# A graph-attention layer on one core: b1 and b2 spread by TensorE, the second table built before the third tile's masks, half of its scaled x on GpSimd

## The chip, the cores and the metric

The kernel runs on one core of a Trainium2 chip. The time is the device time of one execution in microseconds (us). Below, PE is TensorE, DVE is VectorE, ACT is ScalarE, POOL is GpSimd and SP is SyncE, whose queue only starts transfers here.

## The reference, cut to what matters

```python
in_fts = W @ x.T                                  # x: (4096, 128) f32, W: (128, 128)
f1 = (w1 @ in_fts).T + b1                         # (4096, 1)
f2 = (w2 @ in_fts).T + b2                         # (4096, 1)
logits = f1 + f2.T                                # (4096, 4096)
bias = where(adj > 0, 0.0, -1e9)                  # adj: (4096, 4096) int32
coefs = softmax(leaky_relu(logits) + bias, axis=-1)
out = layernorm(x + coefs @ x)                    # (4096, 128) f32, eps 1e-5
```

The adjacency matrix is 64 MiB of int32 and is read once; it is by far the largest operand.

## The kernel before, in words

**The algebra.** The exponential of the leaky ReLU of f1+f2 is exp(f1)exp(f2) where f1+f2 is positive, and exp(0.01 f1)exp(0.01 f2) where it is not. So no 4096 x 4096 matrix of exponentials is made. Two tables are: table 1 holds x scaled by exp(0.01 f2), table 0 holds x scaled by exp(f2), each with the scale itself as one more column, and each as a high f16 half and a low f16 half (258 columns for one block of 128 columns of adj). The coefficients are two masks: mask 1 for the edges of negative sum, mask 0 for those of positive sum. PE multiplies masks by tables.

**A tile** is 128 rows of adj (4096 columns), 32 tiles in all, in slots 0 to 3 (`QT` = 4); four tiles are a quad. For each tile:
- SP and ACT load it (`load_near`, `load_far`: two transfers of 512 KB each). A slot's next load waits for the cast of the tile that is in it (`cast_done`).
- DVE `cast` (L683) makes int8 of the int32 adjacency. ACT `signs` (L445, four activations) writes the signs of f1+f2. DVE `combine` (L688) joins both, DVE `turn` (L696) transposes the mask in blocks of 32 and so gives mask 1, DVE `plus` (L701) makes mask 0.
- PE `edge_sums` (L1002): 32 matmuls of mask 1 with table 1 and 32 of mask 0 with table 0. `turn` of tile t waits for the sums of tile t-4.
- ACT `evacuate` brings the sums out of PSUM. For each quad DVE `moments`, POOL `rows` and ACT `normalise` finish the softmax, the residual and the layer norm, and POOL stores the rows.

**The set-up** ahead of this loop is written out by hand: each engine's list of instructions in the order in which it runs them. x comes in four chunks (`load_x`, `xl_in[h]`). POOL loads w1 and w2 (L340, L341), which PE turns into columns (L969) and multiplies with W (L972, L973). b1 and b2 are loaded by POOL to all 128 partitions (L346, L347). PE transposes x (`turn_x`) and makes f1 (`f1_columns`). DVE makes f2 (`xv_product`, `f2_sum`, one chunk of it on ACT in `f2_sums`), adds b2 (L726), and spreads it as rows (`f2_rows`, L637). `stat_max` and `stat_out`, with PE's `turn_stats` and `widen_stats`, find maxima over all rows.
For each table and each of the four chunks of x: `scale_x` (DVE L667) multiplies the chunk by the scale; `split_x` (ACT L503) writes the high half; `low_x` (DVE L673) the low half. The scaled chunk lies in one buffer, `ybuf`, for both tables: table 0's chunk can be scaled when `low_x` of table 1's has run. Table 0's chunks 0 and 1 are scaled by DVE, 2 and 3 by ACT (`scale_act`, L483: 16 activations).
DVE's order from the first mask on is: mask of tile 0 between the chunks of table 1; `cast`, `combine`, `turn` of tile 1; `cast` and `combine` of tile 2; `scale_x(0, 0)`, `scale_x(0, 1)`, `turn(2, 2)`; `plus` of tiles 0, 1 and 2 between `low_x` of table 0's chunks 0, 1 and 2; tile 3's `cast`, `combine`, `turn`; `low_x(0, 3)`; `plus(3, 3)`.

**The flag.** POOL computes the row factors and then a flag that says whether the fast path may be used (L368 to L392), once the second maxima are there (`gst_ready`). Every engine waits for the flag (`fast`) before it starts with tile 4, so tile 4's `signs` and `cast` come after it. The fast path is the one that runs.

Of the kernel before, what the change touches and what calls it, by code (L numbers as in the profile page):

```python
# [42 lines left out]
def gat_kernel(nc, x, adj, W, w1, b1, w2, b2, out):  # L43
# [24 lines left out]
    with ExitStack() as ctx:  # L68
# [83 lines left out]
        FIRST = 3  # L152
# [124 lines left out]
        def _(sp):  # L277
# [9 lines left out]
            sp.dma_start(wsb[0:P // 2, :], W[0:P // 2, :]).then_inc(w_in, 16)  # L287
            for a in range(A // 2):
                load_x(sp, a, 0)
            for h in range(1, BCH):  # L290
# [47 lines left out]
        def _(pool):  # L338
            pool.memset(ident[:, :], 0.0).then_inc(ident_zero, 1)
            pool.dma_start(wrow[0:1, :], w1).then_inc(w12_in, 16)  # L340
            pool.dma_start(wrow[1:2, :], w2).then_inc(w12_in, 16)  # L341
# [4 lines left out]
            pool.dma_start(b12[:, 0:1], b1.partition_broadcast(P)).then_inc(b12_in, 16)  # L346
            pool.dma_start(b12[:, 1:2], b2.partition_broadcast(P)).then_inc(b12_in, 16)  # L347
# [84 lines left out]
        def _(act):  # L432
            act.dma_start(wsb[P // 2:P, :], W[P // 2:P, :]).then_inc(w_in, 16)
            for h in range(BCH):
                for a in range(A // 2, A):
# [20 lines left out]
            def f2_sums(n0, n1):  # L456
                act.wait_ge(xv_ready, 1)
                for n in range(n0, n1):
                    ins = act.activation(junk[:, n * D:(n + 1) * D], xv[:, n * D:(n + 1) * D], ACT.Copy, accum_out=f2raw[:, n:n + 1])
                ins.then_inc(f2raw_act, 1)  # L460
# [69 lines left out]
            load_far(3, 3)  # L530
            xT_out(6)
            split_x(1, 0)
            xT_out(7)
# [92 lines left out]
        def _(dve):  # L626
# [97 lines left out]
            dve.wait_ge(f2raw_act, 2)
            dve.wait_ge(b12_in, 32)
            dve.tensor_scalar(f2l[:, :], f2raw[:, :], b12[:, 1:2], None, ALU.add).then_inc(f2l_ready, 1)  # L726
            dve.wait_ge(f2l_ready, 1)
# [3 lines left out]
            stat_max(0, 0, 2)  # L731
            dve.wait_ge(consts_ready, 2)
            spread_f1(0, 0, FIRST * KB, 6, 256)
            stat_out(0, 0, 2)
            dve.tensor_scalar(nF2[:, :], gst[:, 0:1], -1.0, None, ALU.mult).then_inc(nF2_ready, 1)
# [382 lines left out]
```

## Time and profile before

| | us |
|---|---|
| median of 3 runs | 285.12 (284.54 to 285.3) |
| profiled execution, its own time | 286.38 |
| its span, first to last instruction | 284.7 |

| engine | busy us | share | instructions |
|---|---|---|---|
| PE matmul | 260.4 | 91% | 2161 |
| DVE | 247.1 | 87% | 320 |
| ACT | 198.3 | 70% | 300 |
| POOL | 70.6 | 25% | 93 |

The mean granted TensorE clock is 0.974 of full. A row of the timeline has start, duration, engine, line, operation, output<-input, shape and count; instructions of one kind that follow each other are merged in one row, and in brackets stand the idle time ahead of it and what ended that.

### The profile page before, as it was taken

What the parts mean: (1) busy time and instruction counts of PE and PEld (TensorE: products, weight loads), DVE (VectorE), ACT (ScalarE), POOL (GpSimd) and SP (SyncE); (2) the same over time, 40 slices, a digit from 0 to 9 for tenths busy, and PEclk for the clock granted to TensorE, in tenths of its full rate; (3) what the DMA queues carried; (4) which work ended last, traced back from release to release, by engine and by line L of the source; (5) the groups of instructions that cost most, each with busy time, mean ns of one, the idle gap of its engine ahead of it and who ended that gap; (6) DMA issues with size and microseconds to landing.
All of it is one profiled execution on the core that took longest, in us unless ns stands there. A gap on an engine that the chain in (4) does not pass through costs nothing.

```text
span 284.7 us, 5940 instructions
## 1 busy us (share of the span) xinstructions
PE 260.4 (91%) x2161; PEld 225.9 (79%) x2161; DVE 247.1 (87%) x320; ACT 198.3 (70%) x300; POOL 70.6 (25%) x93
## 2 busy tenths in 40 slices
PE   0969959799999999999999999999999999999970
PEld 0959846588888888888888888888888888888850
DVE  1878997993997799999999999999999999999862
ACT  2679799936999999699389928991999196113210
POOL 5000004491000003300460056006500650065340
PEclk9999996799999999999999999999999999999996
DMA  5899999999999999999999999999999999501031
GB/s 169 232 287 315 326 316 268 289 281 235 210 268 328 324 326 322 242 314 334 329 294 345 322 322 249 330 340 342 226 327 323 323 249 342 149 0 37 1 90 23
DMA packets 22702, 73.64 MB, mean 259 GB/s; under 512 B 3232, under 2 KB 4384, under 8 KB 22688
## 3 DMA queue, kind: packets, MB, share of 16 engines
q1 hardware_dynamic: 11280, 35.17, 42.5%
q10 hardware_dynamic: 9936, 34.64, 41.3%
q0 software_dynamic: 1472, 3.67, 4.9%
q8 instruction: 6, 0.10, 0.2%
q14 instruction: 8, 0.07, 0.1%
HBM read 71.37 MB, written 2.10 MB: 258 GB/s over the span
## 4 chain that ended last, share of the span: by engine, by line
DVE 59%; DMA 10%; issue 10%; ACT 8%; POOL 5%; PE 3%; ACTq 2%; DVEq 1%; POOLq 0%
DVE mn L683 19%; DVE msk L696 11%; DVE mn L688 10%; DMA nat<-in_adj 7%; ACT sgn L445 6%; DMA msk<-in_x 3%; DVE post L802 3%; DVE ybt L817 2%; PE ps L1002 2%; DVE bns L822 2%; DVE post L804 2%; DVE ntot L807 2%; DVE bt L673 1%; ACTq L268 1%; POOL mrow L371 1%
## 5 line engine op out<-in xcount | busy, mean ns | idle before, releaser
L1002 PE MATMUL ps<-bt,msk 128*128 128x258 f16 x2048 | 236.0, 277 | 5.2 <-DVE msk L696 5.2
L1002 PEld LDWEIGHTS ps<-bt,msk 128*128 128x128 fp8e5 x2048 | 203.2, 99 | 37.5 <-issue 5.5
L445 ACT ACTIVATE sgn<-f2b,nf1l 128x1024 int8<-128x1024 f32 x128 | 136.6, 1144 | 5.7 <-POOL flag L392 4.4
L683 DVE TENSOR_SCALAR mn<-nat 128x4096 int8<-128x4096 int32 x32 | 73.0, 2282 | 7.0 <-DMA nat<-in_adj 4.3
L399 POOL TENSOR_SCALAR nmr<-mv 128x4 f32<-128x4 f32 x7 | 12.6, 1801 | 150.6 <-DVE mv L826 150.6
L688 DVE SCALAR_TENSOR_TENSOR mn<-sgn,mn 128x1024 uint32<-128x1024 uint32 x32 | 39.2, 1225 | 3.4 <-ACT sgn L445 2.4
L696 DVE STREAM_TRANSPOSE msk<-mn 128x1024 uint32<-128x1024 uint32 x32 | 39.8, 1245 | 2.6
L576 ACT ACTIVATE post<-ps,ac 128x258 f32<-128x258 f32 x64 | 26.5, 467 | 22.1 <-PE ps L1002 22.1
L583 ACT ACTIVATE ybt<-ybt,nmr,rstd 128x128 f32<-128x128 f32 x28 | 11.5, 483 | 34.1 <-POOL nmr L404 34.1
L701 DVE TENSOR_SCALAR msk<-msk 128x1024 uint32<-128x1024 uint32 x32 | 22.2, 695 | 1.0
L410 POOL DMA_DIRECT2D out<-ybt x24 | 21.7, 911 | 4.0 <-issue 3.8
L962 PEld LDWEIGHTS ps<-vsb,xn 128*128 128x128 f32 x64 | 14.4, 332 | 0.5 <-issue 0.4
L962 PE MATMUL ps<-vsb,xn 128*128 128x1 f32 x64 | 14.0, 342 | 0.0
L363 POOL DMA_DIRECT2D xn<-in_x x4 | 3.2, 797 | 39.8 <-DVE mn L683 39.8
L673 DVE SCALAR_TENSOR_TENSOR bt<-bt,post 128x1024 f16<-128x1024 f16 x8 | 9.8, 1219 | 0.7 <-ACT bt L503 0.7
L503 ACT ACTIVATE bt<-post 128x1024 f16<-128x1024 f32 x8 | 8.4, 1053 | 2.2 <-DVE post L667 2.1
L817 DVE SCALAR_TENSOR_TENSOR ybt<-ntot,rec,xn 128x128 f32<-128x128 f32 x28 | 8.0, 346 | 1.8 <-DVE rec L811 1.7
L802 DVE TENSOR_TENSOR post<-post 128x1032 f32<-128x1032 f32 x7 | 8.6, 1226 | 0.0
L953 PE MATMUL ps<-ident,msk 128*128 128x128 f32 x32 | 8.5, 427 | 0.0
L400 POOL TENSOR_SCALAR vpe<-mv 128x4 f32<-128x4 f32 x7 | 7.4, 1055 | 0.4
L402 POOL TENSOR_TENSOR rstd<-vpe,mhalf 128x4 f32<-128x4 f32 x7 | 7.3, 1046 | 0.6
L667 DVE TENSOR_TENSOR post<-msk,cs 128x1024 f32<-128x1024 f32 x6 | 7.3, 1213 | 0.0
(106 smaller groups left out, 107.3 us busy)
## 6 DMA issues: line engine op xcount, KB each, us to landing
nat<-in_adj SPq DMA_DIRECT2D x64, 512.0 KB, 13.2
nat<-in_adj ACTq DMA_DIRECT2D x64, 512.0 KB, 16.1
xn<-in_x POOLq DMA_DIRECT2D x4, 512.0 KB, 19.5
out<-ybt POOLq DMA_DIRECT2D x24, 64.0 KB, 7.7
msk<-in_x ACTq DMA_DIRECT2D x8, 128.0 KB, 5.9
msk<-in_x SPq DMA_DIRECT2D x8, 128.0 KB, 4.3
out<-ybt SPq DMA_DIRECT2D x4, 64.0 KB, 2.2
out<-post SPq DMA_DIRECT2D x16, 16.0 KB, 1.5
```

Of the source, the lines that this page charges most:

```text
L410: pool.dma_start(out_g[q, g], ybt[g * SQ:(g + 1) * SQ, s]).then_inc(out_stored[s], 16)
L445: ins = act.activation(sgn[:, c, g * JA:(g + 1) * JA], f2b[:, :], ACT.Sign, bias=nf1l[:, bass.ds(G * t + g, 1)], scale=-1.0)
L576: ins = act.activation(post[:, s, m, c, :], ps[:, 2 * c + m, 0:2 * DV], ACT.Copy, scale=ac[:, m, bass.ds(QT * q + c, 1)])
L673: dve.scalar_tensor_tensor(out=btv[m][:, part, DV:DV + D], in0=btv[m][:, part, 0:D], scalar=-LOW, in1=ybuf[:, h], op0=ALU.mult, op1=ALU.ad ...
L683: dve.tensor_scalar(mn[:, c % 2], nat[:, c], 0, EDGE, ALU.is_gt, ALU.mult).then_inc(cast_done, 1)
L688: dve.scalar_tensor_tensor(out=mn_w[c % 2], in0=sgn_w[c], scalar=MINUS, in1=mn_w[c % 2], op0=ALU.bitwise_xor, op1=ALU.bitwise_and).then_in ...
L696: dve.transpose(turned[c].rearrange("p (b g s) -> p g b s", b=NB, g=G), mn_w[c % 2].rearrange("p (g b r) -> p g b r", g=G, b=NB)).then_inc ...
L701: dve.tensor_scalar(plus_w[c], turned[c], PLUS, 1, ALU.bitwise_and, ALU.logical_shift_right).then_inc(plus_ready, 1)
L802: dve.tensor_tensor(post[:, s, 0], post[:, s, 0], post[:, s, 1], ALU.add).then_inc(sums_added, 1)
L817: dve.scalar_tensor_tensor(out=ybt[:, s, c, :], in0=ntot[:, c, 0:D], scalar=rec[:, c:c + 1], in1=xn[:, bass.ds(QT * q + c, 1), :].rearrang ...
L962: ins = pe.matmul(ps[:, bank, at:at + 1], xT[:, n * P:(n + 1) * P], vsb[:, D:D + 1], start=True, stop=True)
L1002: ins = pe.matmul(ps[:, 2 * c + m, 0:2 * DV], mask_f[c][m][:, n // KB, n % KB, :], btv[m][:, n, :], start=(n == 0), stop=(n == NK - 1))
```

## The change

- w1 and w2 are loaded on ACT's queue ahead of its x chunks; W is one transfer on SP's queue. b1 and b2 are loaded by POOL to one partition (`brow`), and PE spreads them with a matmul by a row of ones; DVE copies the result (`b12`).
- `f1_columns` of the first two blocks (`FIRST` = 2, was 3) multiplies with both vectors, so f2 of chunk 0 comes from PE too; DVE's product and ACT's eight sums for that chunk (`f2_sums`) are gone.
- In the set-up, the first exponential on ACT comes ahead of `square(2)`, the second one behind `signs` of tile 0; DVE runs `spread_f1` of the first rows ahead of `f2_rows`, and `scale_x(1, 1)` ahead of tile 0's cast.
- Table 0's chunks 0 and 1 are scaled by POOL (one 128x1024 multiplication each, signal `y_act`), 2 and 3 by DVE; `scale_act` is gone.
- Table 0 is finished (DVE and ACT) before `cast`, `combine` and `turn` of tile 2 and `signs` of tile 2 begin. PE runs mask 0 of tiles 0 and 1 with all of table 0, and then mask 1 and mask 0 of tile 2.
- POOL's load of x by rows (`xn`) waits for the cast of tile 1, was that of tile 2.

```diff
-        FIRST = 3
+        FIRST = 2
+        F2_AT = FIRST * KB
...
-            pool.dma_start(wrow[0:1, :], w1).then_inc(w12_in, 16)
-            pool.dma_start(wrow[1:2, :], w2).then_inc(w12_in, 16)
+            pool.dma_start(brow[:, 0:1], b1.partition_broadcast(1)).then_inc(brow_in, 16)
+            pool.dma_start(brow[:, 1:2], b2.partition_broadcast(1)).then_inc(brow_in, 16)
...
-            pool.dma_start(b12[:, 0:1], b1.partition_broadcast(P)).then_inc(b12_in, 16)
-            pool.dma_start(b12[:, 1:2], b2.partition_broadcast(P)).then_inc(b12_in, 16)
...
+            pool.wait_ge(cs_ready[0], 1)
+            for h in range(2):
+                pool.wait_ge(table_ready[1], h + 1)
+                part = slice(h * CN, (h + 1) * CN)
+                pool.tensor_tensor(ybuf[:, h], xl_chunk(h), cs[:, 0, part, None].to_broadcast([P, CN, D]),
+                                   ALU.mult).then_inc(y_act, 1)
...
-            pool.wait_ge(cast_done, 3)
+            pool.wait_ge(cast_done, 2)
...
@@ ACT, after signs of tile 1 @@
-            rows_out()
-            signs(2, 2, between=next_tile)
-            square(3)
-            act.wait_ge(nf1l_ready, 2)
-            signs(3, 3, between=lambda: split_x(0, 0))
-            act.wait_ge(cast_done, 3)
-            load_far(QT + 2, 2)
-            split_x(0, 1)
-            scale_act(2)
-            split_x(0, 2)
-            scale_act(3)
-            split_x(0, 3)
+            square(3)
+            rows_out()
+            split_x(0, 0)
+            act.wait_ge(cast_done, 2)
+            load_far(QT + 1, 1)
+            split_x(0, 1)
+            split_x(0, 2)
+            split_x(0, 3)
+            act.wait_ge(nf1l_ready, 2)
+            signs(2, 2)
+            signs(3, 3, between=next_tile)
...
@@ DVE, after combine of tile 1 @@
-            turn(1, 1)
-            cast(2, 2, 0)
             dve.wait_ge(f1n_ready, G)
             dve.tensor_reduce(stat[:, 2:3], f1n[:, :], AX_X, ALU.max, apply_absolute_value=True)
-            combine(2, 2)
             dve.wait_ge(squares_ready, BCH)
             dve.tensor_reduce(stat[:, 3:4], squares[:, :], AX_X, ALU.add).then_inc(stat_ready, 1)
+            turn(1, 1)
             dve.wait_ge(cs_ready[0], 1)
             low_den(0)
-            scale_x(0, 0)
+            scale_x(0, 2)
             stat_max(1, 2, 4)
-            scale_x(0, 1)
-            dve.wait_ge(y_ready[0], 2)
-            turn(2, 2)
+            scale_x(0, 3)
             plus(0, 0)
             low_x(0, 0)
+            plus(1, 1)
             stat_out(1, 2, 4)
-            plus(1, 1)
             low_x(0, 1)
-            plus(2, 2)
             low_x(0, 2)
+            low_x(0, 3)
+            cast(2, 2, 0)
+            combine(2, 2)
+            dve.wait_ge(y_act, 2)
+            turn(2, 2)
+            plus(2, 2)
             cast(3, 3, 0)
             combine(3, 3)
-            dve.wait_ge(y_act, 2)
+            dve.wait_ge(y_ready[0], 2)
             turn(3, 3)
-            low_x(0, 3)
             plus(3, 3)
...
@@ PE, after the first table-1 sums @@
-            edge_sums(1, 1)
-            turn_stats(1, 2, 4)
+            edge_sums(1, 1, 0, NK // 2)
             widen_stats(1, 2, 4)
-            pe.wait_ge(turn_done, 3)
-            edge_sums(2, 1)
+            edge_sums(1, 1, NK // 2, NK)
             pe.wait_ge(den_ready[0], 1)
             pe.wait_ge(xeps_ready, 1)
-            plus_sums(0, range(2))
-            plus_sums(1, range(2))
-            plus_sums(0, [2])
-            plus_sums(1, [2])
-            plus_sums(2, range(3))
+            for h in range(BCH):
+                plus_sums(h, range(2))
+            pe.wait_ge(turn_done, 3)
+            edge_sums(2, 1)
+            for h in range(BCH):
+                plus_sums(h, [2])
```

## Rows read from the trace of the kernel before

**Rows 1.** Windows: from:to, length, busy us (count) by engine, clock, DMA share, GB/s.
```profile
60.00:80.00 20.00, 20.00 (x181) 17.46 (x180) 15.07 (x13) 14.01 (x18) 4.76 (x13) 1.00 1.03 238
```
**Rows 2.** Timeline of the last 35 us: PE's last row, DVE's last `plus`.
```profile
249.79 25.78 PE L1002 MATMUL ps<-bt,msk 128*128 128x258 f16 x229
...
260.72 0.69 DVE L701 TENSOR_SCALAR msk<-msk 128x1024 uint32<-128x1024 uint32 x1
```
**Rows 3.** Timeline of PE alone, 36 to 60 us.
```profile
36.83 2.46 PE L1002 MATMUL ps<-bt,msk 128*128 128x258 f16 x16
42.41 6.46 PE L1002 MATMUL ps<-bt,msk 128*128 128x258 f16 x32 [3.12 <-DVE msk L696]
...
52.09 8.11 PE L1002 MATMUL ps<-bt,msk 128*128 128x258 f16 x59 [2.12 <-DVE msk L696]
```
**Rows 4.** Windows of PE alone: busy us (count), clock, DMA share, GB/s.
```profile
52.00:54.00 2.00, 1.91 (x10) 0.50 1.04 295
```
**Rows 5.** Costliest groups: line, operation, count | busy us, mean ns | idle before.
```profile
L683 DVE TENSOR_SCALAR mn<-nat 128x4096 int8<-128x4096 int32 x32 | 73.0, 2282 | 7.0 <-DMA nat<-in_adj 4.3
...
L688 DVE SCALAR_TENSOR_TENSOR mn<-sgn,mn 128x1024 uint32<-128x1024 uint32 x32 | 39.2, 1225 | 3.4 <-ACT sgn L445 2.4
L696 DVE STREAM_TRANSPOSE msk<-mn 128x1024 uint32<-128x1024 uint32 x32 | 39.8, 1245 | 2.6
...
L701 DVE TENSOR_SCALAR msk<-msk 128x1024 uint32<-128x1024 uint32 x32 | 22.2, 695 | 1.0
...
L673 DVE SCALAR_TENSOR_TENSOR bt<-bt,post 128x1024 f16<-128x1024 f16 x8 | 9.8, 1219 | 0.7 <-ACT bt L503 0.7
L503 ACT ACTIVATE bt<-post 128x1024 f16<-128x1024 f32 x8 | 8.4, 1053 | 2.2 <-DVE post L667 2.1
...
L667 DVE TENSOR_TENSOR post<-msk,cs 128x1024 f32<-128x1024 f32 x6 | 7.3, 1213 | 0.0
```
**Rows 6.** Timeline of DVE's set-up, 15 to 70 us.
```profile
15.13 1.23 DVE L629 TENSOR_TENSOR sgn<-msk,vsb 128x1024 f32<-128x1024 f32 x1 [0.83 <-DMA msk<-in_x]
...
18.11 2.00 DVE L637 STREAM_TRANSPOSE f2b<-f2l 128x1024 f32<-128x1024 f32 x1
...
21.73 1.22 DVE L667 TENSOR_TENSOR post<-msk,cs 128x1024 f32<-128x1024 f32 x1
...
23.27 2.29 DVE L683 TENSOR_SCALAR mn<-nat 128x4096 int8<-128x4096 int32 x1 [0.34 <-DMA nat<-in_adj]
...
29.80 1.24 DVE L696 STREAM_TRANSPOSE msk<-mn 128x1024 uint32<-128x1024 uint32 x1
...
37.44 2.29 DVE L683 TENSOR_SCALAR mn<-nat 128x4096 int8<-128x4096 int32 x1
...
66.57 2.29 DVE L683 TENSOR_SCALAR mn<-nat 128x4096 int8<-128x4096 int32 x1 [2.66 <-issue]
```
**Rows 7.** Timeline of ACT at 18.8 us.
```profile
18.77 0.21 ACT L521 ACTIVATE de<-f2l 128x32 f32<-128x32 f32 x1
```
**Rows 8.** Timeline of the first 7 us, PE.
```profile
6.43 0.23 PE L969 MATMUL ps<-ident,wrow 2*128 2x2 f32 x1 [6.43 <-DMA wrow<-in_L_gnn_w]
```
**Rows 9.** Timeline of POOL alone, 0 to 66 us.
```profile
2.95 0.31 POOL L344 TENSOR_SCALAR_AFFINE_SELECT ident<-ident 128x128 f32<-128x128 f32 x1
...
53.92 2.35 POOL L368 TENSOR_SCALAR gsum<-f1n,gst 128x32 f32<-128x32 f32 x1 [5.67 <-DVE gst L662]
...
56.45 3.18 POOL L371 TENSOR_SCALAR mrow<-gsum 128x32 f32<-128x32 f32 x1
...
61.23 0.25 POOL L377 TENSOR_TENSOR ea<-ea,mrow 128x32 f32<-128x32 f32 x1
61.44 0.19 POOL L379 TENSOR_TENSOR rng<-gst 128x1 f32<-128x1 f32 x1
...
65.21 0.30 POOL L392 TENSOR_SCALAR flag<-rng 128x1 int32<-128x1 f32 x1
```
**Rows 10.** Loads of adj issued from 45 to 60 us.
```profile
DMA to landing us min/median/max: 16.6/20.5/24.5
```

More of the change, by code:

```diff
@@ L285, in load_tile @@
                 load_near(QT * q + c, c)
[L287 to L290, printed above, removed]
+            sp.dma_start(wsb[:, :], W).then_inc(w_in, 16)
+            for h in range(BCH):
                 for a in range(A // 2):
@@ L436, in _ @@
                     load_x(act, a, h)
+                if h == 1:
+                    act.wait_ge(consts_ready, 1)
+                    act.activation(ac[:, 0, 0:1], ones[:, 0:1], ACT.Copy)
             def load_far(t, c):
@@ L454, in xT_out @@
                                accum_out=xt8[:, b:b + 1]).then_inc(xT_ready, 1)
[L456 to L460, printed above, removed]
             def square(h):
                 act.wait_ge(xl_in[h], 16 * A)
-                if h == 0:
-                    act.wait_ge(f2raw_act, 2)
-                else:
+                if h:
                     act.wait_ge(squares_ready, h)
@@ L530, in _ @@
             load_far(3, 3)
+            split_x(1, 0)
             xT_out(6)
-            split_x(1, 0)
-            xT_out(7)
+            act.wait_ge(nF2_ready, 1)
+            act.activation(be[:, :], f2l[:, :], ACT.Exp, bias=nF2[:, 0:1]).then_inc(exp_ready, 1)
+            scales(0, be)
             split_x(1, 1)
@@ L715, in _ @@
             dve.wait_ge(vsb_ready, 1)
-            xv_product(0)
             xv_product(1)
             f2_sum(1)
+            dve.wait_ge(b12_made, 1)
+            dve.tensor_copy(b12[:, :], ps[:, 6, D + 2:D + 4]).then_inc(b12_ready, 1)
             xv_product(2)
             f2_sum(2)
+            dve.wait_ge(b12_ready, 1)
+            dve.wait_ge(f1_made, 1)
+            dve.tensor_scalar(f2l[:, 0:F2_AT], ps[:, 0, F2_AT:2 * F2_AT], b12[:, 1:2], None,
+                              ALU.add).then_inc(f2l_ready, 1)
+            dve.wait_ge(consts_ready, 2)
+            spread_f1(0, 0, FIRST * KB, 0, 0)
             xv_product(3)
@@ L723, in _ @@
             dve.wait_ge(f2raw_ready, BCH - 1)
[L724 to L727, printed above, removed]
+            dve.tensor_scalar(f2l[:, F2_AT:], f2raw[:, F2_AT:], b12[:, 1:2], None, ALU.add).then_inc(f2l_ready, 1)
+            dve.wait_ge(f2l_ready, 2)
             dve.tensor_reduce(stat[:, 0:1], f2l[:, :], AX_X, ALU.max)
@@ L730, in _ @@
             f2_rows()
[L731 to L735, printed above, removed]
             dve.wait_ge(nf1_made, 1)
@@ L740, in _ @@
             scale_x(1, 0)
+            stat_max(0, 0, 2)
+            scale_x(1, 1)
+            stat_out(0, 0, 2)
+            dve.tensor_scalar(nF2[:, :], gst[:, 0:1], -1.0, None, ALU.mult).then_inc(nF2_ready, 1)
             cast(0, 0, 0)
             low_den(1)
-            scale_x(1, 1)
             combine(0, 0)
@@ L977, in _ @@
             f1_columns(0)
+            pe.wait_ge(brow_in, 32)
+            pe.matmul(ps[:, 6, D + 2:D + 4], ones[0:1, :], brow[:, :], start=True, stop=True).then_inc(b12_made, 1)
             turn_x(2)
@@ L981, in _ @@
             f1_columns(2)
-            turn_stats(0, 0, 2)
-            turn_x(4)
-            widen_stats(0, 0, 2)
             pe.wait_ge(alike_ready, 1)
@@ L989, in _ @@
                       stop=True).then_inc(nf1_made, 1)
+            turn_x(4)
+            turn_stats(0, 0, 2)
             f1_columns(3)
+            widen_stats(0, 0, 2)
             turn_x(5)
@@ L1040, in _ @@
             edge_sums(2, 1)
-            pe.wait_ge(den_ready[0], 1)
-            pe.wait_ge(xeps_ready, 1)
-            plus_sums(0, range(2))
-            plus_sums(1, range(2))
-            plus_sums(0, [2])
-            plus_sums(1, [2])
-            plus_sums(2, range(3))
+            for h in range(BCH):
+                plus_sums(h, [2])
             pe.wait_ge(gst_ready, 2)
@@ L1053, in _ @@
             edge_sums(3, 1)
-            plus_sums(3, range(3))
             for h in range(BCH):
```

64 lines of the change are left out of this document (31 added, 33 removed).

## The prediction

> **What bounds the kernel now.** I read the windows first, then the end of the timeline, then PE's restart, then the set-up's order. In a window of the main loop PE is busy all of its 20 us at full clock, and the DMA engines are full too [rows 1]. At the end DVE has made its last mask at 260.72 + 0.69 = 261.4, while PE works until 249.79 + 25.78 = 275.57 [rows 2]: a backlog of 14 us. The chain of waits names DVE most, because `turn` waits for sums of four tiles before, but what sets the end is PE. PE's last idle time of its own ends at 52.09 [rows 3]; from there it never stops. By the program 64 matmuls of L1002 lie before 52.09 (mask 1 of tiles 0 and 1; 16 + 32 of them are in the first two of [rows 3]), so 1984 of 2048 lie behind it. The clock was 0.50 until about 54 [rows 4], which costs half of 2 us. So one matmul takes (275.57 - 52.09 - 1.0)/1984 = 0.1121 us, a tile of 64 takes 7.17.
>
> So the question is when PE's unbroken stretch starts and how much is left then. I count from the start of tile 2's mask-1 sums in the new order, where 2048 - 128 = 1920 matmuls are left: 1920 x 0.1121 = 215.2 us. Before, that much was left at 275.57 - 215.2 = **60.35**. Call the same point after S. The time changes by S - 60.35, if nothing starves PE later. The tail behind 275.57 is untouched. The profiled execution took 286.38 us with a span of 284.7; the median of the runs is 285.12, and I apply the difference to the median.
>
> **The front, to tile 1's cast.** PE's first instruction waited until 6.43 for w1 and w2 [rows 8]. On ACT's queue they come earlier, by some 2 us, and the spread of b1 and b2 is one matmul and one copy. I cost all this at nothing: DVE's f2 of the last chunk starts at 15.13 when x lands [rows 6], and that covers it. If the cover were gone it would be worth 2 us at most. ACT's x loads are issued one descriptor list later (some 0.5 us); if x lands later by that, it is a loss of 0 to 0.5, taken as 0. W as one transfer changes nothing that is waited for.
>
> From 15.13 the sums and maxima are as before, so `f2_rows` ends at 18.11 + 2.00 = 20.1 [rows 6]. The first exponential started at 18.77 behind `square(2)` [rows 7]; it now runs at 18.0, so `scale_x(1, 0)` starts at 20.35 and not at 21.73 [rows 6]. Two `scale_x` (1.21 each) and the maxima (about 0.9) then bring DVE to 23.65 for tile 0's cast, which could not start before 23.27, when its load landed [rows 6]. Most of the gain is then given back: `combine(0)` waits for `signs` of tile 0, which starts 1.4 us earlier but now has PE's `turn_x(5)` behind `widen_stats` in its middle; I get 26.5 for its end, and 26.5 to 27.55 for `split_x(1, 0)` (1.05, [rows 5]). `low_x(1, 0)` follows (1.22), and `turn(0)` starts at 28.9, before at 29.80 [rows 6]. Then the same list as before, with ACT's second exponential (0.8) now in the way of `split_x(1, 3)`: tile 1's cast would start at **37.0**, before at 37.44 [rows 6].
>
> **POOL's two multiplications.** No POOL instruction of this size is in the trace. From `affine_select`, 0.31 for 128 elements [rows 9], 1024 elements would take 2.5; from 0.25 for 32 elements against 0.19 for one [rows 9], 0.19 + 1024 x 0.0019 = 2.1. I take 2.2 each. The first can start when the second exponential and `low_x(1, 0)` are done, at 29.0; the second after `low_x(1, 1)`. What they do to DVE the trace shows from one side only: L368 (32 elements) took 2.35 and L371 3.18 where the neighbour of the same size, L377, took 0.25 [rows 9], and in their time DVE ran `low_x`, `plus` and `cast` at their usual durations. So POOL waits for DVE whole instructions long. Whether DVE waits for POOL no row shows; the bounds are 0 and all of the 2 x 2.2 us. I take the same whole-instruction wait, since it is the only kind of conflict the rows have. During `turn` and the reductions POOL went on (L377 at 61.23 lies in tile 3's `turn` and took its 0.25, [rows 9]), so those cover it. The first runs 29.0 to 31.2, covered by `turn(0)` to 30.15: `scale_x(1, 2)` starts 1.0 late. The second gets in at 36.0, between `low_x(1, 2)` and `spread_f1`, is covered for 0.45 and delays `low_x(1, 3)` to 38.2. Tile 1's cast then starts at **39.4**: 2.4 behind 37.0 and 2.0 behind today's.
>
> The Trainium skill ("SBUF — State Buffer", section "SBUF: two separate sides") has the shared port pair as an exclusive lock held for a whole instruction by whichever of the two started first. By that rule the sum is the one just made; by bandwidth sharing it would lie between this and rival A. The rows agree for POOL's half of it. The skill's "GPSIMD Engine Reference", section 3, gives 4497 ns for a two-input add of 2048 elements; an estimate from it is 2.2 us for 1024.
>
> **From tile 1's cast to S.** DVE in order: cast 2.28, combine 1.23, two small reductions 0.3, turn 1.25, `low_den` 0.3, `scale_x` 1.21, `stat_max` 0.5, `scale_x` 1.21, plus 0.69, `low_x` 1.22, plus 0.69, `stat_out` 0.15, three `low_x` 3.66, then tile 2's cast 2.28, combine 1.23, turn 1.25 [rows 5]. Sum 19.5. The small reductions wait for ACT's rows, behind `signs(1)` and `square(3)`; ACT has them out by 41.5, in time. ScalarE loses its 16 scaling activations, which were off the path. S = 39.4 + 19.5 = **58.9**. PE must have done mask 0 of tiles 0 and 1 by then: table 0's first chunk is ready at 49.6 and the last at 54.1, and 64 matmuls at 0.112 take 7.2, so PE is through by 58. It works at half clock from turn(1) on for about 6 us, as in the row of 42.41 (6.46 us for 32) [rows 3], and that is covered, as it was before. `turn(3)` ends 5.5 after S, PE needs it at S + 7.17.
>
> **Behind S.** PE needs tile 4's `turn` at S + 14.34 = 73.2 (before: 74.7). Tile 4 hangs on the flag: flag at 65.51 [rows 9], four `signs`, `combine`, `turn` gave 73.36, that is flag + 7.86. POOL's chain now starts at S - 8.5 = 50.4 and meets three `low_x` and a cast, 5.9 us in which it stands still; then `turn(2)` and `turn(3)` let it through. I get the flag at S + 6.4 = 65.3, `turn(4)` at 73.2: just in time, 0.0 to 0.3 late. Tile 4's cast waited for the flag too, at 66.57 [rows 6]. Tile 2's cast moves from 42.2 to some 54.2, so tile 6's loads are issued 12 us later on SP's and ACT's queues, at 56.5. PE needs that mask at S + 28.7, DVE must begin it by 82.8: 26 us, against 24.5 for the slowest load of that stretch [rows 10]. Just covered. The load `xn` is issued a few us earlier, nobody waits for it before 100.
>
> **The sum:** S 58.9 against 60.35 is -1.45, the flag +0.15: **-1.3 us, 283.8 us**. This case's own range is 282.7 to 284.9.
>
> **Rivals.**
> A. DVE does not wait for POOL. Then cast(1) starts at 37.0, S = 56.5, -3.8 us: 281.3. For it: POOL's instructions never lengthened a DVE instruction in the trace. Against: none of them was longer than 0.3 us of own work. Chance 0.20.
> B. The other side: the flag becomes the bound. Its chain of 18 small POOL instructions took from 53.92 to 65.51 [rows 9], with DVE idle or in port-free work for much of the last 4 us. It now sits between the back-to-back `low_x`, casts and combines. If one more cast (2.3 us) gets ahead of it, the flag comes at 68, `turn(4)` ends at 75.9, and PE starts tile 4 1.2 us later than before: 286.3. It decides from a flag at 66.8 on (no gain), and from 67.7 on the kernel is slower by 0.3%. Tile 6's load coming 2 us late would look alike in time but not in place. Chance 0.18.
> C. The change does not do what it says: x lands 0.5 late and POOL's multiplications take 3 us, so each stall grows by 0.8; S is 61, flat: 284.4 to 285.9, centre 285.4. Chance 0.17.
>
> **How the numbers follow.** Forecast 0.45, A 0.20, B 0.18, C 0.17. A measurement here tells about 0.3%, 0.86 us, from no change. The forecast lies beyond that with seven eighths of its chance; with A that is 0.59 faster. Same: the rest of the forecast, most of C, some of B: 0.23. Slower: B's larger part: 0.18. The range takes in A and B: 281.2 to 286.5.
>
> **What would show it.** `scale_x(1, 2)` (the third L667 of the set-up) starting over 1 us behind `turn(0)`, while a POOL multiplication ends at its start, shows the stall; back to back shows A. The start of tile 1's cast near 39.4, `turn(2)` ending near 58.9 with PE idle 1 us or less before it, and PE without idle from there on, show the sum. A gap in PE at tile 4 (near 73) with ACT's `signs` behind L392 shows B; a gap at tile 6 shows the load. It is wrong if PE's mask-0 sums of tiles 0 and 1, at half clock, end behind `turn(2)`.

## The result, and the profile after

The changed kernel takes **280.75 us** (median; 280.48 to 282.38), beside 285.21 (284.54 to 287.0) for the kernel before on the same chip: a ratio of 0.985, interval 0.981 to 0.990. A second measurement on another chip gave 0.981 (0.977 to 0.985). The forecast of 283.8 had the right sign and was too small by 3 us, and 280.75 lies below its range.

The profiled execution has a span of 278.8 us and 280.48 us as its own time, 5.9 less than that of before. The medians differ by 4.5, because before's profiled execution was 1.2 above its median. So single times of the traces explain the gain up to about 1.4 us, not better.

First, three groups of the changed kernel's page, as in [rows 5].

```profile
L363 POOL TENSOR_TENSOR post<-msk,cs 128x1024 f32<-128x1024 f32 x2 | 4.7, 2352 | 24.5 <-DVE bt L664 24.5
...
L664 DVE SCALAR_TENSOR_TENSOR bt<-bt,post 128x1024 f16<-128x1024 f16 x8 | 11.3, 1433 | 0.0
...
L658 DVE TENSOR_TENSOR post<-msk,cs 128x1024 f32<-128x1024 f32 x6 | 8.1, 1351 | 0.0
```

The mean of `low_x` rose from 1219 ns to 1433 and that of `scale_x` from 1213 to 1351 [rows 5]: 8 x 0.214 + 6 x 0.138 = 2.5 us.

Next, PE alone in the changed kernel, which answers to [rows 2, 3], and its windows (columns as in [rows 4]).

```profile
35.41 3.09 PE L1003 MATMUL ps<-bt,msk 128*128 128x258 f16 x16
...
40.92 3.60 PE L1003 MATMUL ps<-bt,msk 128*128 128x258 f16 x16 [0.87 <-DVE msk L687]
...
44.96 224.73 PE L1003 MATMUL ps<-bt,msk 128*128 128x258 f16 x2000
```

```profile
44.00:46.00 2.00, 2.00 (x10) 0.50 1.03 270
46.00:48.00 2.00, 2.00 (x19) 0.94 1.01 274
```

PE's unbroken stretch starts at 44.96, before at 52.09. Of its 2000 matmuls 80 lie ahead of tile 2's. Counted back from 44.96 + 224.73 = 269.69, the other 1920 begin at 269.69 - 215.2 = **54.5** = S. It was 60.35 before and was forecast at 58.9. The 215.2 us for 1920 matmuls can be checked in e6 below, where PE waits right ahead of tile 2's sums and so shows them as one row (in brackets the wait for `turn(2)`):

```profile
53.20 214.96 PE L1008 MATMUL ps<-bt,msk 128*128 128x258 f16 x1920 [1.28 <-DVE msk L692]
```

The clock column has PE at the lower level (0.50) until about 46.

DVE's set-up in the changed kernel, in start times, answers to [rows 6]:

```profile
12.88 1.22 DVE L620 TENSOR_TENSOR sgn<-msk,vsb 128x1024 f32<-128x1024 f32 x1
...
17.73 1.21 DVE L658 TENSOR_TENSOR post<-msk,cs 128x1024 f32<-128x1024 f32 x1
...
20.83 2.29 DVE L674 TENSOR_SCALAR mn<-nat 128x4096 int8<-128x4096 int32 x1
...
26.25 1.24 DVE L687 STREAM_TRANSPOSE msk<-mn 128x1024 uint32<-128x1024 uint32 x1
27.41 2.05 DVE L658 TENSOR_TENSOR post<-msk,cs 128x1024 f32<-128x1024 f32 x1
29.39 1.22 DVE L664 SCALAR_TENSOR_TENSOR bt<-bt,post 128x1024 f16<-128x1024 f16 x1
30.52 1.21 DVE L658 TENSOR_TENSOR post<-msk,cs 128x1024 f32<-128x1024 f32 x1
31.66 2.92 DVE L664 SCALAR_TENSOR_TENSOR bt<-bt,post 128x1024 f16<-128x1024 f16 x1
...
35.92 2.28 DVE L674 TENSOR_SCALAR mn<-nat 128x4096 int8<-128x4096 int32 x1
...
53.10 1.25 DVE L687 STREAM_TRANSPOSE msk<-mn 128x1024 uint32<-128x1024 uint32 x1
...
67.66 1.25 DVE L687 STREAM_TRANSPOSE msk<-mn 128x1024 uint32<-128x1024 uint32 x1
```

And POOL alone in the changed kernel: its two multiplications and the flag.

```profile
26.49 1.90 POOL L363 TENSOR_TENSOR post<-msk,cs 128x1024 f32<-128x1024 f32 x1 [22.24 <-DVE bt L664]
30.68 2.81 POOL L363 TENSOR_TENSOR post<-msk,cs 128x1024 f32<-128x1024 f32 x1 [2.30 <-DVE bt L664]
...
60.77 0.30 POOL L399 TENSOR_SCALAR flag<-rng 128x1 int32<-128x1 f32 x1
```

Step by step, with start times:

| step | before | forecast | measured |
|---|---|---|---|
| last f2 product | 15.13 | 15.13 | 12.88 |
| `scale_x(1, 0)` | 21.73 | 20.35 | 17.73 |
| tile 0's cast | 23.27 | 23.65 | 20.83 |
| `turn(0)` | 29.80 | 28.9 | 26.25 |
| tile 1's cast | 37.44 | 39.4 | 35.92 |
| S | 60.35 | 58.9 | 54.5 |
| flag done | 65.51 | S + 6.4 | S + 6.6 |

The first rows are 2.3 to 2.8 us ahead of the forecast. Behind `turn(0)` some 0.8 us more comes in up to tile 1's cast, and 0.9 from there to S, so that S is 4.4 ahead. The larger part is there before `turn(0)`. So the first question for the experiments was: what moved the front?

The row to look at is the share of time in which the DMA engines were busy, while x lands. The kernel before, DMA view of the first 12 us in 40 slices of 0.3 us (each digit tenths), then the changed kernel:

```profile
DMA  0000000056957999999998943122557999999999
...
msk<-in_x ACTq DMA_DIRECT2D x8, 128.0 KB, 5.9
...
b<-in_L_gnn_b POOLq DMA_DIRECT2D x2, 0.5 KB, 6.1
```

```profile
DMA  0000000659878989999999999999999999999999
...
msk<-in_x ACTq DMA_DIRECT2D x8, 128.0 KB, 4.3
...
brow<-in_L_gnn_b POOLq DMA_DIRECT2D x2, 0.0 KB, 3.4
```

Before, from 6.9 to 9.0 us the engines fell to 1 to 5 tenths with all of x and the first masks still to come. In the changed kernel there is no dip. The last number of the load rows is us from issue to landing.

### The profile page after: what moved, and what is told of

It reads as the page before. It is cut to its first block, busy times and chain, and to the rows that moved or that the text cites. A ratio compares the mean times of both kernels' runs of the same rounds, so it can differ in the third digit from the quotient of the medians.

```text
span 278.8 us, 5912 instructions
## 1 busy us (share of the span) xinstructions
PE 259.6 (93%) x2163; PEld 225.5 (81%) x2163; DVE 248.3 (89%) x321; ACT 191.0 (69%) x268; POOL 78.3 (28%) x93
## 4 chain that ended last, share of the span: by engine, by line
DVE 66%; issue 9%; DMA 8%; POOL 6%; ACT 5%; ACTq 2%; DVEq 1%; PE 1%; POOLq 0%
DVE mn L674 20%; DVE msk L687 11%; DVE mn L679 11%; DMA nat<-in_adj 7%; ACT sgn L456 5%; DVE post L797 3%; DVE bt L664 2%; DVE ybt L812 2%; DVE post L658 2%; DVE bns L817 2%; DVE post L799 2%; DVE ntot L802 2%; DMA msk<-in_x 2%; DVE f2raw L624 1%; DVE sgn L620 1%
## 5 line engine op out<-in xcount | busy, mean ns | idle before, releaser
L456 ACT ACTIVATE sgn<-f2b,nf1l 128x1024 int8<-128x1024 f32 x128 | 136.6, 1147 | 10.3 <-POOL flag L399 6.4
L567 ACT ACTIVATE post<-ps,ac 128x258 f32<-128x258 f32 x64 | 26.6, 469 | 19.3 <-PE ps L1003 19.2
L417 POOL DMA_DIRECT2D out<-ybt x24 | 22.3, 935 | 3.4 <-issue 3.3
L363 POOL TENSOR_TENSOR post<-msk,cs 128x1024 f32<-128x1024 f32 x2 | 4.7, 2352 | 24.5 <-DVE bt L664 24.5
L664 DVE SCALAR_TENSOR_TENSOR bt<-bt,post 128x1024 f16<-128x1024 f16 x8 | 11.3, 1433 | 0.0
L960 PEld LDWEIGHTS ps<-vsb,xn 128*128 128x128 f32 x48 | 10.9, 332 | 0.3 <-ACT xn L464 0.3
L960 PE MATMUL ps<-vsb,xn 128*128 128x1 f32 x48 | 10.4, 338 | 0.2 <-ACT xn L464 0.2
L464 ACT ACTIVATE xn<-ps 128x512 f32<-128x512 f32 x8 | 4.7, 592 | 5.1 <-PE ps L948 5.1
L658 DVE TENSOR_TENSOR post<-msk,cs 128x1024 f32<-128x1024 f32 x6 | 8.1, 1351 | 0.0
```

What stands on the lines that cost most here:

```text
L417: pool.dma_start(out_g[q, g], ybt[g * SQ:(g + 1) * SQ, s]).then_inc(out_stored[s], 16)
L456: ins = act.activation(sgn[:, c, g * JA:(g + 1) * JA], f2b[:, :], ACT.Sign, bias=nf1l[:, bass.ds(G * t + g, 1)], scale=-1.0)
L567: ins = act.activation(post[:, s, m, c, :], ps[:, 2 * c + m, 0:2 * DV], ACT.Copy, scale=ac[:, m, bass.ds(QT * q + c, 1)])
L658: dve.tensor_tensor(ybuf[:, h], xl_chunk(h), cs[:, m, part, None].to_broadcast([P, CN, D]), ALU.mult).then_inc(y_ready[m], 1)
L664: dve.scalar_tensor_tensor(out=btv[m][:, part, DV:DV + D], in0=btv[m][:, part, 0:D], scalar=-LOW, in1=ybuf[:, h], op0=ALU.mult, op1=ALU.ad ...
L960: ins = pe.matmul(ps[:, 7, n - F2_AT:n - F2_AT + 1], xT[:, n * P:(n + 1) * P], vsb[:, D:D + 1], start=True, stop=True)
```

## The experiments

Two theories for the front (theory 1 and theory 2 in the expectations of e1 to e3). **Theory S**: the loads of b1 and b2 to 128 partitions, 256 elements of 4 bytes, hold the DMA engines up, and so hold x up. **Theory Q**: it is w1 and w2 on ACT's queue (PE's first matmul now at 3.38, before 6.43 [rows 8]). For the two multiplications of POOL, **theory L** (a lock for whole instructions, both ways) against **theory P** (DVE is not affected; the "rival P" in e6's expectation is another one, that PE sets the start of the unbroken stretch). Each chip of the experiments had its own runs of the kernel before, with medians from 285.88 to 286.28; numbers from different chips are compared by their ratio to it.

**e1: only b1 and b2 changed, in the kernel before.**

```diff
-pool.dma_start(b12[:, 0:1], b1.partition_broadcast(P))
-pool.dma_start(b12[:, 1:2], b2.partition_broadcast(P))
+pool.dma_start(brow[:, 0:1], b1.partition_broadcast(1))
+pool.dma_start(brow[:, 1:2], b2.partition_broadcast(1))
...
+pe.matmul(ps[:, 2, 0:2], ones[0:1, :], brow[:, :], start=True, stop=True)
+dve.tensor_copy(b12[:, :], ps[:, 2, 0:2])
```

> The kernel before, and only b1 and b2 changed: loaded to one partition instead of 128 and spread by a PE matmul and a DVE copy. x's last chunk lets DVE start its f2 product at 15.13 us in the trace before and at 12.88 in the changed kernel. Theory 1 (the two loads of b to 128 partitions, 4 bytes each, hold the DMA engines up at 6 to 10 us, where their share was 0.60 to 0.68): the product starts near 13, the DMA share at 6 to 10 us is over 1.0, and the time falls by 1.5 to 2.3 us, to some 283.3. Theory 2 (the earlier x comes from w1, w2 and W on other queues): the product stays at 15.1 and the time within 0.4 us of the kernel before.

**e2: the reverse, in the changed kernel** (POOL loads b1 and b2 to 128 partitions, PE's matmul and DVE's copy go).

> The changed kernel with b1 and b2 loaded to 128 partitions by GpSimd again, no spread by PE, all else as changed. Theory 1: the last f2 product goes back from 12.88 to about 15, the start of tile 1's cast from 35.9 to about 38, and 1.5 to 2.3 us of the gain of 4.4 are lost (282.3 to 283). Theory 2: nothing moves by more than 0.4 us.

e1 took 283.92 us, ratio 0.993 (0.989 to 0.996). e2 took 283.25, ratio 0.992 (0.989 to 0.994), where the changed kernel had 0.985 and 0.981. The windows (as in [rows 4], here with all engines) of e1, then of e2:

```profile
6.00:8.00 2.00, 1.44 (x7) 1.38 (x8) 0.31 (x2) 1.12 (x2) 0.00 (x0) 1.00 1.02 315
```

```profile
4.00:6.00 2.00, 0.30 (x3) 0.21 (x1) 0.29 (x1) 1.10 (x2) 0.20 (x1) 1.00 0.56 184
6.00:8.00 2.00, 1.75 (x8) 1.57 (x8) 0.00 (x0) 0.59 (x2) 0.00 (x0) 1.00 0.38 138
```

The dip is gone in e1 (share 1.02) and back in e2 (0.56 and 0.38), where POOL issues the loads. In e2 DVE's timeline has its first f2 product waiting 4.96 us for x; the second row is tile 1's cast, 1.8 us later than in the changed kernel:

```profile
9.59 1.23 DVE L617 TENSOR_TENSOR sgn<-msk,vsb 128x1024 f32<-128x1024 f32 x1 [4.96 <-DMA msk<-in_x]
...
37.71 2.28 DVE L671 TENSOR_SCALAR mn<-nat 128x4096 int8<-128x4096 int32 x1
```

So S holds in both directions. But in e1 the last f2 product moved only from 15.13 to 14.48, not to 12.88: something more is in the front.

**e3: w1 and w2 back on POOL's queue and W in halves, in the changed kernel.**

```diff
-act.dma_start(wrow[0:1, :], w1)
-act.dma_start(wrow[1:2, :], w2)
+act.dma_start(wsb[P // 2:P, :], W[P // 2:P, :])
...
+pool.dma_start(wrow[0:1, :], w1)
+pool.dma_start(wrow[1:2, :], w2)
```

> The changed kernel with w1 and w2 on GpSimd's queue ahead of b1 and b2, and W in two halves on SP's and ACT's queues, as in the kernel before. Theory 1: PE's first instruction goes from 3.4 back to about 6.4 us, hidden behind the x loads for most of it: DVE's last f2 product moves by 0 to 0.7 us, the time by 0 to 0.7. Theory 2: the product goes back to 15, the time rises by 2.

It took 282.45, ratio 0.989 (0.983 to 0.995): by the ratios 1.2 to 2.3 us more than the changed kernel, though the intervals overlap; S is at 55.87, 1.4 later. No dip in the DMA share (1.06 and over from 4 us on), yet the last f2 product came at 14.25, 1.4 later, and tile 0's cast at 23.02. Neither theory had this size: theory S expected 0 to 0.7 us, theory Q 2. What moved the cast stands in ACT's queue. The timeline of e3 has ACT's first transfer of tile 0's load and DVE's cast of that tile; then come the same issue in the kernel before, with the activation at its start, and both in the changed kernel:

```profile
8.12 0.65 ACTq L277 DMA_DIRECT2D nat<-in_adj  x1
...
23.02 2.30 DVE L675 TENSOR_SCALAR mn<-nat 128x4096 int8<-128x4096 int32 x1 [0.87 <-DMA nat<-in_adj]
```

```profile
8.93 0.60 ACT L453 ACTIVATE xn<-ps 128x512 f32<-128x512 f32 x1 [1.79 <-PE ps L953]
8.93 0.65 ACTq L274 DMA_DIRECT2D nat<-in_adj  x1
```

```profile
6.74 0.60 ACT L464 ACTIVATE xn<-ps 128x512 f32<-128x512 f32 x1 [1.63 <-PE ps L948]
6.75 0.70 ACTq L277 DMA_DIRECT2D nat<-in_adj  x1
```

ACT issues this load right at its first `xn` activation, which has waited for PE. With w1 and w2 late, PE is late, and so is the load. In e1 the issue was at 8.81 and the cast at 23.75, still waiting for the load. From this issue to the start of the cast it is 14.3 us before and 14.9 in e1 and e3; the whole front below has 14.1. So the landing of tile 0 follows PE's start. (No run moved this issue and nothing else; that it decides is read from these rows.)

**e5: the whole new front alone, in the kernel before** (b1 and b2 to one row, w1 and w2 on ACT's queue, W as one transfer, x chunks in order; nothing of the new order, no POOL multiplications).

> The kernel before, with all loads of the front as in the changed kernel (w1 and w2 on ACT's queue, W in one transfer, b1 and b2 to one partition and spread by PE), and its old order behind. Theory F (front and order each bring about half): against the kernel before it gains 2 to 2.8 us (283.3 or less where before is 285.9), since b alone gave 2.0; PE's unbroken stretch starts near 50.3. Rival (the order alone brings nearly all, and the front's gain is swallowed by the wait for tile 0's load, which b alone already met with 1.46 us of idle time): no more than 2.0, and DVE's wait for that load grows to 2 us.

It took 282.5, ratio 0.989 (0.985 to 0.993): 3.4 us, more than expected. PE's unbroken stretch starts at 48.38 (before 52.09), where 50.3 was expected. DVE's timeline, its last f2 product and tile 0's and tile 1's casts, 2.5, 2.3 and 2.6 us ahead of [rows 6]:

```profile
12.59 1.21 DVE L629 TENSOR_TENSOR sgn<-msk,vsb 128x1024 f32<-128x1024 f32 x1
...
20.96 2.29 DVE L683 TENSOR_SCALAR mn<-nat 128x4096 int8<-128x4096 int32 x1 [0.58 <-DMA nat<-in_adj]
...
34.82 2.29 DVE L683 TENSOR_SCALAR mn<-nat 128x4096 int8<-128x4096 int32 x1
```

**e9: the changed kernel with both front parts undone** (the edits of e2 and e3 together), which leaves the new order, the work moved off DVE for chunk 0, and POOL's multiplications.

> The changed kernel with both parts of its front undone (w1, w2 and the 128-row b1, b2 on GpSimd's queue, W in halves): what the new order, the shorter f2 and GpSimd's multiplications bring alone. The front alone brought 3.4 us of 285.9. Theory F (front and order add up): 1.0 to 2.2 us faster than the kernel before in the same job. Rival (they overlap, since both end at the wait for tile 0's load): over 3 us faster, or no faster at all.

It took 284.61, ratio 0.995 (0.991 to 0.998): 1.6 us. PE alone in e9 shows S at 58.10, and DVE's first f2 product waits for x:

```profile
58.10 4.08 PE L997 MATMUL ps<-bt,msk 128*128 128x258 f16 x35 [1.57 <-DVE msk L685]
```

```profile
11.43 1.23 DVE L618 TENSOR_TENSOR sgn<-msk,vsb 128x1024 f32<-128x1024 f32 x1 [3.88 <-DMA msk<-in_x]
```

e5's 1.1% and e9's 0.55% add up to 1.6%; the changed kernel gained 1.5% and 1.9%. But e9 is not quite "the order with the old front": its x landed later than before (DMA share 0.35 and 0.53 in 6:8 and 8:10 us, before 0.60 and 0.68), and its last f2 product came at 16.50, where it was 15.13. Against the changed kernel that is 3.6 us, and S differs by 3.6 us too.

**e10: b1 and b2 to 128 partitions again, but on ACT's queue ahead of its x chunks.** This asks whether GpSimd's queue has a part in the dip.

```diff
-pool.dma_start(b12[:, 0:1], b1.partition_broadcast(P))
-pool.dma_start(b12[:, 1:2], b2.partition_broadcast(P))
...
+act.dma_start(b12[:, 0:1], b1.partition_broadcast(P))
+act.dma_start(b12[:, 1:2], b2.partition_broadcast(P))
```

> The changed kernel with b1 and b2 loaded to all 128 partitions, but on ACT's queue behind w1 and w2 instead of GpSimd's. With them on GpSimd's queue the DMA share fell to 0.56 and 0.38 in 4:6 and 6:8 us. Theory K (GpSimd's queue, software-made packets, holds the DMA engines up): the share stays at 1.0 and the time is within 0.5 us of the changed kernel. Theory S (it is the 256 packets of 4 bytes, whichever queue they come from): the share falls below 0.8 in some 2 us of 4 to 10, x lands 1 to 2 us late, and the time is 1.5 to 2.5 us above the changed kernel's.

It took 285.36, ratio 0.998 (0.994 to 1.001), 3.9 us above the changed kernel on the same chip (281.45, **e11** below). The dip is as deep, and the first f2 product waits 6.42. DMA view of e10's first 12 us, and DVE's row:

```profile
DMA  0000002567294420002355999999999999999999
```

```profile
11.10 1.22 DVE L617 TENSOR_TENSOR sgn<-msk,vsb 128x1024 f32<-128x1024 f32 x1 [6.42 <-DMA msk<-in_x]
```

It is the loads and not GpSimd's queue. That it came out worse than on POOL's queue was expected by neither theory in size. Two things add up here: x on SP's queue, which has no b in front of it, took 6.0 us from issue to landing, as in e2 (5.9); x on ACT's queue took 7.0 (e2: 6.2) and was issued from 2.69 on (e2: 1.75), behind b1 and b2. ACT's first `xn` activation, and with it tile 0's load, came at 10.70 (e2: 7.41).

**e4: DVE scales the two chunks, POOL none. e6: ScalarE scales them, POOL none. e8: POOL does each multiplication twice.** All in the changed kernel.

```diff
-pool.tensor_tensor(ybuf[:, h], xl_chunk(h), cs[:, 0, part, None]..., ALU.mult)
+scale_x(0, 0); scale_x(0, 1)     # e4, on DVE
+scale_act(0) ... scale_act(1)    # e6, on ACT, behind rows_out()
+pool.tensor_tensor(...); pool.tensor_tensor(...)    # e8
```

> The changed kernel without GpSimd's two multiplications: DVE scales chunks 0 and 1 of table 0 too, right ahead of its chunks 2 and 3. Theory L (DVE and GpSimd exclude each other for a whole instruction): the two lengthened DVE instructions (2.05 instead of 1.21, 2.92 instead of 1.22) go back to 1.2, tile 1's cast starts 2.5 us earlier (33.4), turn of tile 1 too, and DVE then spends 2.42 more on its own: turn of tile 2 ends within 0.3 of now, and the time is the same within 0.5 us. Rival (the two were long for another reason, PE or ACT's writes): they stay long, and the time rises by 2.4 us, to 283.2.

> The changed kernel, but ScalarE scales table 0's chunks 0 and 1 (16 activations, 4.9 us, behind the row sums), and GpSimd multiplies nothing. Theory L (GpSimd's two multiplications cost DVE 0.84 + 1.70 us of stall): tile 1's cast starts near 34.0, as with DVE scaling, and DVE has no added work, so turn of tile 2 ends near 52.2 instead of 54.35 and PE is through 1.7 to 2.3 us earlier: 278.4 to 279.0. Rival P (PE, not DVE, sets the start of the unbroken stretch, or ScalarE becomes late): turn of tile 2 is earlier but the time stays within 0.5 us of 280.8; or combine of tile 2 waits for ScalarE's signs.

> The changed kernel with each of GpSimd's multiplications done twice (the same result): four of 1.9 to 2.8 us. Theory L (whoever has the port keeps it for a whole instruction): four DVE instructions are lengthened by 0.8 to 1.7 us each, 5.5 to 6 us in all where it was 2.5, tile 1's cast starts near 39.4 instead of 35.9, and the time rises by 3 to 3.5 us, to 284. Rival (the engines share, or DVE only loses while it starts): the stalls stay at 2 to 3 us in all, GpSimd's own instructions get longer, and the time rises by less than 1 us.

| kernel | us | ratio, interval | lengthening of DVE's four | tile 1's cast | S |
|---|---|---|---|---|---|
| changed | 280.75 | 0.985 (0.981 to 0.990) | 0.84 + 1.70 | 35.92 | 54.5 |
| e4 | 281.62 | 0.988 (0.981 to 0.994) | 0 | 33.97 | 54.73 |
| e6 | 278.99 | 0.977 (0.971 to 0.983) | 0 | 33.97 | 53.20 |
| e8 | 284.45 | 0.999 (0.996 to 1.002) | 0.84 + 1.70 + 1.69 + 1.40 | 39.10 | 57.67 |

DVE's timeline in e6 at the places where the changed kernel stalled, and then the same in e8:

```profile
27.50 1.18 DVE L663 TENSOR_TENSOR post<-msk,cs 128x1024 f32<-128x1024 f32 x1
28.60 1.22 DVE L669 SCALAR_TENSOR_TENSOR bt<-bt,post 128x1024 f16<-128x1024 f16 x1
```

```profile
27.48 2.05 DVE L662 TENSOR_TENSOR post<-msk,cs 128x1024 f32<-128x1024 f32 x1
29.46 2.92 DVE L668 SCALAR_TENSOR_TENSOR bt<-bt,post 128x1024 f16<-128x1024 f16 x1
...
33.43 2.91 DVE L668 SCALAR_TENSOR_TENSOR bt<-bt,post 128x1024 f16<-128x1024 f16 x1
...
36.56 2.62 DVE L668 SCALAR_TENSOR_TENSOR bt<-bt,post 128x1024 f16<-128x1024 f16 x1
```

Two multiplications lengthen two DVE instructions, four lengthen four, and without any none is longer: theory L. P is out. POOL alone in e8 shows the other half:

```profile
26.56 1.90 POOL L364 TENSOR_TENSOR post<-msk,cs 128x1024 f32<-128x1024 f32 x1 [22.31 <-DVE bt L668]
28.54 2.75 POOL L367 TENSOR_TENSOR post<-msk,cs 128x1024 f32<-128x1024 f32 x1
```

The one that begins in `turn(0)` takes 1.90, one that begins in a `scale_x` 2.75. The second has waited about 0.9 for DVE's instruction to end (28.54 + 0.9 = 29.4, where DVE's next begins, 29.46), and then DVE waits until 28.54 + 2.75 = 31.3 and runs its 1.2. They take turns, whole instructions at a time.

The Trainium skill ("SBUF — State Buffer", section "SBUF: two separate sides") calls this an exclusive lock. These rows agree, now for both engines: DVE's `low_x` takes 1.22 free and 2.92 behind a multiplication.

What POOL saves DVE in e4's terms is two `scale_x` (2.4 us), and what it costs DVE is 2.54 of stalls. Of these 1.95 reach tile 1's cast (35.92 against 33.97), since `low_x(1, 3)` no longer waits 0.45 for ACT. S is 54.73 without POOL's help and 54.5 with it, and the intervals of the ratios overlap: the help is worth nothing measurable here. Given to ScalarE instead, the work is free of stalls. In e6 `turn(2)` ended at 53.06 and not at 52.2 as expected: DVE waited 0.40 us for `split_x` and 0.32 for `signs`, so ScalarE was a little late.

**e7 and e12 (the same kernel on two chips), e11 (the changed kernel again):** e6 with `square(2)` ahead of the first exponential and `square(3)` in `square(2)`'s place, so that ACT has less to do ahead of `rows_out`.

> The kernel with ScalarE scaling both chunks, and its sums of squares moved into its idle time ahead of the first exponential, which takes 1.24 us off ScalarE behind signs of tile 1. If ScalarE is what combine of tile 2 or low_x waits for, this gains another 0.5 to 1.2 us (277.5 to 278.3); if not, it is the same within 0.3, or 0.3 later by a later exponential.

> The changed kernel itself, on the chip of this job, so that the others of this job can be set against it: ratio to the kernel before 0.982 to 0.988.

> The kernel in which ScalarE scales table 0's chunks 0 and 1 and makes its squares early, again, beside the changed kernel: 1.5 to 2.5 us below it. If the earlier ratio (0.9753) was chance, it is within 1 us of the changed kernel.

e7 took 278.68, ratio 0.975 (0.969 to 0.982), and e12 279.01, ratio 0.974 (0.970 to 0.977); e11 took 281.45, ratio 0.981 (0.977 to 0.985), just below the 0.982 to 0.988 that was expected. On one chip e12 is 2.4 us below the changed kernel and 7.3 below before, the best of the versions here. The order of the squares by itself (e7 against e6: 0.3 us) is too small to tell.

## Why the prediction was wrong, step by step

- **What failed is the step "the front costed at nothing".** It read `[0.83 <-DMA msk<-in_x]` at 15.13 [rows 6] as a cover of fixed place: x lands when it lands, and whatever comes earlier in front of it is hidden. But the landing itself depended on the edit, through the 256 small elements of b1 and b2 (e1, e2, e10). The same holds for the second cover that the prediction named, tile 0's load at 23.27. Its issue on ACT's queue stands behind PE's first work, and moved from 8.93 to 6.75 with w1 and w2 (e1 and e3 against e5). With both gone, `scale_x(1, 0)` came 2.6 us ahead of the forecast. The prediction did say "2 us at most" if the cover went; e5 measured 3.4 (interval 2.0 to 4.2; by its trace PE's stretch starts 3.7 earlier). Rival C had x landing 0.5 late; it landed early. Rival A's 281.3 is nearer to the measured time than the forecast, but its mechanism did not occur: DVE did wait.
- **The rest of the change was forecast nearly right, in part by luck.** e9 is the run nearest to what the prediction assumed: 1.6 us gained (interval 0.5 to 2.7) where 1.3 was forecast, tile 1's cast at 39.55 for 39.4, S at 58.10 for 58.9. But two errors cancel in it. Its `turn(0)` came at 29.87, 1.0 behind the forecast, since x landed late; from there to tile 1's cast it took 9.7 us where 10.5 was forecast, and from there to the end of `turn(2)` 18.4 where 19.5 was.
- **From `turn(0)` to tile 1's cast; POOL's multiplications: mechanism right, sizes nearly, one place wrong.** The forecast was 8.1 us without stalls and 2.4 of stalls. e6, without stalls, has 7.6 (26.34 to 33.97): the 0.5 for the second exponential in the way of `split_x(1, 3)` did not show, since `low_x(1, 3)` waited 0.45 there and 0.47 before. The stalls came to 2.0: the two instructions were longer by 0.84 and 1.70, less the 0.45. The second was expected to slip in behind `low_x(1, 2)` and delay `low_x(1, 3)`. It was issued at 30.68, within a `scale_x`, and got in between that and `low_x(1, 2)`, though the two follow each other with no gap. Rival A fell. POOL's own time was 1.90 where I took 2.2.
- **From tile 1's cast to S** 19.5 was forecast, and DVE needed 54.35 - 35.92 = 18.4. DVE starts an instruction before the end of the one ahead of it (`turn(0)` ends at 27.49, the next starts at 27.41; the `low_x` at 29.39 ends at 30.61, the next starts at 30.52): 0.08 to 0.09 for each such pair. The durations of these 20 instructions add up to 19.3 in the changed kernel's own trace, so 0.9 of the 1.1 is this overlap. The prediction's sums should have been made from start to start.
- **The clause of mask 0.** The prediction said it was wrong if PE's mask-0 sums ended behind `turn(2)`. `turn(2)` ended at 54.35; PE worked without a break from 44.96 and came to tile 2's sums at 54.5, 0.15 behind it, so the two bounds met. PE was not idle there, while in e4, e6 and e9 it waited 0.64, 1.28 and 1.57 for `turn(2)`. By this an earlier `turn(2)` alone would not have moved S in the changed kernel; no run tried that alone.
- **Behind S.** The flag was done at 61.07 = S + 6.6, close to the forecast S + 6.4, and `turn(4)` ended at 68.91 = S + 14.4, with PE needing it at S + 14.34. The window 60:80 has PE at 19.94 of 20 us. Rival B's mechanism is there and costs no more than 0.3 us, as forecast; it did not become the bound. (The flag's chain is 17 instructions in the rows and not 18.) No gap of PE at tile 6 showed.
- **"What sets the end is PE" no longer holds in every execution.** e11 is the changed kernel too; its profiled execution took 283.57, 3.1 more than that of the first, though PE's stretch starts only 0.4 later (45.33, there 44.96). In it DVE waited for three loads of adj in a row (2.84, 1.43 and 1.48 us; in the first trace 0.28, 1.99 and 1.19), and PE then for DVE ahead of tile 10. At the end the last sums were evacuated at 272.33, but DVE came to them only at 273.79, with no idle time in front; in the first trace the two fell together (270.57 and 270.60), and in the kernel before DVE had waited 0.83 us for them. From the last matmul to the end of the span it is 9.1 us before and in the first trace, and 10.5 in e11. Three rows of e11, and the one of the kernel before:

```profile
83.76 2.29 DVE L674 TENSOR_SCALAR mn<-nat 128x4096 int8<-128x4096 int32 x1 [2.84 <-DMA nat<-in_adj]
...
273.79 0.42 DVE L851 TENSOR_TENSOR post<-post 128x258 f32<-128x258 f32 x1
```

```profile
113.77 157.68 PE L1003 MATMUL ps<-bt,msk 128*128 128x258 f16 x1408 [1.24 <-DVE msk L687]
```

```profile
276.48 0.43 DVE L856 TENSOR_TENSOR post<-post 128x258 f32<-128x258 f32 x1 [0.83 <-ACT post L576]
```

From the last of these waits to its last cast DVE takes about the same time in each trace: 155.6 us before (100.13 to 255.77), 155.7 in the first trace and 156.2 in e11. So with S 5.9 us earlier, PE and DVE end nearly together, and what DVE waits for loads near 80 to 100 us can now reach the time. By these traces that is part of the spread of single executions (280.28 to 283.57 in e11), and S alone does not give a run's time: the part behind the last matmul is 10.3 us in e5's trace, 10.0 in e9's and 11.2 in e3's.

The 4.5 us then are 3.4 of front and 1.6 of order by e5 and e9 (their intervals, some 1.1 us each way, cover the difference of the sum, 5.0, from 4.5).

**Left open.** Why 256 elements of 4 bytes keep 16 engines from other work for 2 to 4 us is not shown by any row, only that they do, from two queues. How much of the higher cost from ACT's queue is the later issue of x and how much the longer dip is open too. e3's own size (1.2 to 2.3 us) is not resolved. Why e9's x landed later than before's, with the same loads of b1 and b2, is open too, and so is whether DVE's wait for the loads near 80 to 100 us can be shortened.

## What to carry to other kernels

A row that says "waits for a load" is no fixed cover: ask what the load's landing and its issue depend on, and whether the edit touches that; a dip in the DMA share while loads are outstanding is the sign. Don't load a scalar to 128 partitions in the opening; load it to one and let PE spread it. A two-input multiplication on GpSimd beside a busy DVE cost DVE nearly the time that it takes on GpSimd (1.4 to 1.7 us for 1.9), and less where it began in a transpose (0.84); so first look for room on ScalarE. And when a stage is shortened, look again at what sets the end: here DVE came level with PE.

## What was not expected of the hardware

- Two loads of 4 bytes to each of 128 partitions: DMA share 0.18 to 0.68 over some 4 us in place of 1.0 to 1.1, and 2.0 us of the kernel's time (e1) to 3.9 (e10).
- With w1 and w2 on ACT's queue PE's first matmul began at 3.38, and by its row waited for `ident` and no longer for them; from POOL's queue it was 6.43. That is at least 3 us, where 2 was taken. In e2, where `ident` was ready sooner, it began at 2.80 and did wait for them.
- A multiplication on GpSimd of 128x1024 f32 took 1.90 us unhindered and 2.75 to 2.81 where it had to wait; it gets its turn between two DVE instructions with no gap between them.
- Most of DVE's back-to-back instructions start 0.08 to 0.09 us before the end of the one before. The Trainium skill ("Perfetto Trace Analysis", section "Optimizing Scalar/DVE Operations") has a fixed access time of some 60 ns in SBUF, twice that in a profiled latency, since the acknowledgement of the write lies beside the next instruction. The rows agree in kind; they have 80 to 90 ns where an estimate from the page's figure is some 60.
